# The cross loop's order on TensorE: the attended pair directly behind the third scores, and what follows from it

## What is computed

```python
z = _mha(x1, context, Wq2, Wk2, Wv2, mask1, causal=False)   # 16 heads of 32
x2 = _layernorm(x1 + z, ln2_g, ln2_b)
z = jnp.maximum(x2 @ fc1_w.T + fc1_b, 0.0) * mask0
z = (z @ fc2_w.T + fc2_b) * mask0
return _layernorm(x2 + z, ln3_g, ln3_b)
```

## Time and profile before

| | us |
|---|---|
| median of 3 runs | 2673.7 (2673.52 to 2676.07) |
| the profiled execution, its own time | 2674.73 |
| its span in the trace | 2673.0 |
| TensorE busy in the span | 2629.6 (98%) |
| VectorE busy in the span | 1911.7 (72%) |

### The profile page before, as it was taken

The page is one execution under the profiler, slowest core; times in us unless marked ns, Lnnn a source line. Parts: engine busy times, 40 slices in busy tenths (PEclk is TensorE's granted clock), DMA queues, the critical chain, the costliest instruction groups (busy, mean ns, idle before and its releaser), DMA issues.

```text
span 2673.0 us, 66075 instructions
## 1 busy us (share of the span) xinstructions
PE 2629.6 (98%) x22888; PEld 2268.3 (85%) x22888; DVE 1911.7 (72%) x5311; ACT 1546.2 (58%) x4774; POOL 744.7 (28%) x943
## 2 busy tenths in 40 slices
PE   7999999999999999999999999999999999999997
PEld 6888888887888888888888888888788888888886
DVE  7777877776534443444478888887788888888877
ACT  6777777777211111111267777777676776767764
POOL 3333343330100000000103333333442434424342
PEclk9999999999999999999999999999999999999998
DMA  4333334252211211022121111112321322213210
GB/s 157 119 121 98 110 111 127 87 156 78 89 54 41 61 36 60 31 63 63 48 96 48 47 47 47 47 47 79 100 80 63 98 67 71 86 63 99 66 50 23
DMA packets 180500, 202.54 MB, mean 76 GB/s; under 512 B 17616, under 2 KB 107728, under 8 KB 179536
## 3 DMA queue, kind: packets, MB, share of 16 engines
q1 hardware_dynamic: 180432, 201.66, 23.6%
HBM read 137.65 MB, written 63.96 MB: 75 GB/s over the span
## 4 chain that ended last, share of the span: by engine, by line
PE 93%; DVE 4%; ACT 2%; issue 1%; DMA 0%; POOL 0%; DVEq 0%; ACTq 0%; POOLq 0%
PE cross_work L172 17%; PE mlp_acc L3137 13%; PE mlp_f L3119 13%; PE mask_work L172 13%; PE causal_work L172 10%; PE cross_scores L2146 3%; PE mask_scores L2146 3%; PE cross_scores L2123 2%; PE causal_scores L2146 2%; PE mask_attended L2173 2%; PE cross_attended L2173 2%; PE mask_scores L2123 2%; PE causal_scores L2123 2%; PE causal_attended L2173 2%; PE cross_probsT L2146 1%; PE mask_probsT L2146 1%
## 5 line engine op out<-in xcount | busy, mean ns | idle before, releaser
L2915 ACT ACTIVATE mlp_h<-mlp_f,mlp_b1col 128x512 f32<-128x512 f32 x128 | 88.3, 690 | 526.1 <-PE mlp_f L3119 526.0
L3119 PE MATMUL mlp_f<-mlp_xT_hi,mlp_w 128*128 128x512 f32 x1024 | 335.4, 389 | 0.2 <-DVE mlp_xT_lo L3006 0.2
L3020 DVE CAST mlp_hT_hi<-mlp_h 128x512 fp32r<-128x512 f32 x128 | 58.1, 454 | 369.9 <-ACT mlp_h L2915 369.8
L3137 PE MATMUL mlp_acc<-mlp_w,mlp_hT_hi 128*128 128x512 f32 x1024 | 315.2, 389 | 0.0
L888 ACT ACTIVATE mask_prob<-mask_scores,mask_low 128x256 f32<-128x256 f32 x512 | 236.0, 486 | 66.0 <-DVE mask_low L1445 64.7
L888 ACT ACTIVATE cross_prob<-cross_scores,cross_low 128x256 f32<-128x256 f32 x512 | 237.3, 490 | 63.3 <-DVE cross_low L1439 63.3
L888 ACT ACTIVATE causal_prob<-causal_scores,causal_low 128x128 f32<-128x128 f32 (+1 forms) x512 | 210.4, 437 | 93.4 <-DVE causal_low L1445 93.4
L3119 PEld LDWEIGHTS mlp_f<-mlp_xT_hi,mlp_w 128*128 128x128 f32 x1024 | 192.1, 188 | 40.8 <-DVE mlp_xT_lo L3006 0.6
L1445 DVE CUSTOM_DVE_ANT_0 mask_scores<-mask_scores,mask_mask 128x256 f32<-128x256 f32 x512 | 198.6, 461 | 38.5 <-PE mask_scores L2123 27.7
L3137 PEld LDWEIGHTS mlp_acc<-mlp_w,mlp_hT_hi 128*128 128x128 f32 x1024 | 192.2, 188 | 39.8
L172 PE MATMUL causal_work<-causal_xT_hi,causal_w 128*128 128x256 f32 x1008 | 217.0, 293 | 0.3 <-DVE causal_qk_parts L1404 0.3
(11 more groups left out here) (350 smaller groups left out, 7808.9 us busy)
## 6 DMA issues: line engine op xcount, KB each, us to landing
cross_x_in<-after_attention SPq DMA_DIRECT2D x17, 512.0 KB, 4.1
mask_x_in<-in_x SPq DMA_DIRECT2D x16, 512.0 KB, 4.3
mask_c_in<-in_ctx SPq DMA_DIRECT2D x16, 512.0 KB, 5.2
mask_res<-in_x SPq DMA_DIRECT2D x16, 512.0 KB, 3.6
after_attention<-mask_res SPq DMA_DIRECT2D x16, 512.0 KB, 2.8
mlp_x<-after_attention SPq DMA_DIRECT2D x8, 1024.0 KB, 5.7
mlp_stage<-in_L_xattn_fc_w SPq DMA_DIRECT2D x8, 1024.0 KB, 5.6
after_layer<-mlp_y SPq DMA_DIRECT2D x8, 1024.0 KB, 4.3
```

The source lines that it names most:

```text
L2915: act.activation(h32[:, m % 2, :], F1[m % 2][:], ACT.Gelu, bias=b1col[:, m:m + 1]).then_inc(s["gelu"], 1)
L3119: ins = pe.matmul(F1[m % 2][:], W[2 * (m // 4)][:, a, k, m % 4 * P:(m % 4 + 1) * P], xT[p][:, k, :], start=(k == 0 and n == 0), stop=(k == ...
L3137: ins = pe.matmul(ACC[t][:], hT[a][:, m % 2, t * P:(t + 1) * P], W[2 * (m // 4) + 1][:, p, m % 4, :], start=(m == 0 and n == 0), stop=(m = ...
```

## The change

On TensorE the second values are made whole (twelve matmuls) between turn_probs(b,6) and turn_probs(b,7). The attended pair, attend(b,0,2), is issued directly behind scores(b,2), ahead of post_turn. The second post_turn writes bank W0, where the values stood, and not O; its wait is now for v_ready. turn_probs(b,8) and (b,9) stand ahead of feed1(b,0,(0,)), turn_probs(b,10) behind it. ScalarE takes values(b,1) directly behind turned(b+1,1), then exps(b,8), exps(b,9), and only then post_hi(b,0) and post_hi(b,1). VectorE makes the four minima of chunk 2 in one go ahead of post_lo, where two stood on either side. The turn of b = 0 keeps its work, with a small reordering; in cross_end the first of the four banks becomes O for W0.

```diff
-    POST_BANK = (W1, O) if cross else (SC[2], O)
+    POST_BANK = (W1, W0) if cross else (SC[2], O)
...
-    END_BANK = (W0, PT, SC[2], SC[3])
+    END_BANK = (O, PT, SC[2], SC[3])
...                                  (ScalarE, cross_turn)
-            if not prev:
-                values(b, 1)
-            if prev:
-                post_hi(b, 0)
-                post_hi(b, 1)
+            values(b, 1)
             if cur:
                 exps(b, 8)
-                if prev:
-                    values(b, 1)
...
                 exps(b, 9)
...
+                if prev:
+                    post_hi(b, 0)
+                    post_hi(b, 1)
                 exps(b, 10)
                 exps(b, 11)
                 copy(b, 8)
...                                  (VectorE, cross_turn)
-                minima(b, 2, (0, 1))
+                minima(b, 2)
             if prev:
                 post_lo(b, 0)
                 post_lo(b, 1)
-            if cur:
-                minima(b, 2, (2, 3))
...                                  (TensorE, cross_turn)
                 pe.wait_ge(s["v_ready"], 2 * b + 1)
-                values(b, 1, 0)
+                values(b, 1)
...
                 turn_probs(b, 7)
                 scores(b, 2)
+                attend(b, 0, 2)
...
                 post_turn(b - 1, 0)
-                pe.wait_ge(s["z_done"], KC * b + 1)
+                pe.wait_ge(s["v_ready"], 2 * b + 2)
                 post_turn(b - 1, 1)
             if cur:
                 energies0(b, 3)
-                if prev:
-                    values(b, 1, 1)
-
+            if cur and not prev:
+                pe.wait_ge(last["z_done"], KC * B + 1)
+                attend(b, 0, 2)
+            if cur:
+                turn_probs(b, 8)
+                turn_probs(b, 9)
             if prev:
                 feed1(b, 0, (0,))
             if cur:
-                if not prev:
-                    pe.wait_ge(last["z_done"], KC * B + 1)
-                attend(b, 0, 2)
-                turn_probs(b, 8)
+                turn_probs(b, 10)
             if prev:
                 feed1(b, 0, (1,))
-            if cur:
-                turn_probs(b, 9)
-
-            if cur:
-                turn_probs(b, 10)
-            pe.wait_ge(s["v_ready"], 2 * b + 2)
-            if prev:
                 feed1(b, 1, (0,))
                 attended(b, 0, 2)
                 feed1(b, 1, (1,))
```

## The result

The changed kernel takes 2727.43 us (median of 4 runs, 2726.42 to 2728.93) against 2673.93 us (4 runs, 2673.52 to 2676.07) for the kernel before: a ratio of 1.0197, with a 95% interval of 1.0185 to 1.0209 (the two medians alone give 1.0200). The prediction was 2727.3. Its span is 2726.4 us, 53.4 more than before.

The account below looks back on a forecast made before the run. TensorE was taken as full, with a path through VectorE equally long. The longer path's 3.8 us for b = 1 to 13, plus 3.0 and 1.2, summed to 53.6 us: 2727.3 us, range 2697 to 2738.

Parts of the forecast that it names:

- Two paths of equal length: TensorE's own list, and post_turn through post_hi and VectorE's list to qk_lo and queries(b+1,1), both close a turn, 0.07 us apart.
- TensorE's own list: TensorE's stream, full at 47.73 us a turn before; predicted to grow 1.7 us a turn.
- the path through VectorE: From the first post_turn through VectorE's list to queries(b+1,1): 3.8 us a turn longer, bounds 2.7 and 4.2.
- The three waits: New TensorE waits each turn: at attend 0.6 us, at feed1 for post_lo 0.4, at the attended pair's transposes 0.8.
- What VectorE is late with: TensorE waits at turn_probs(b,12), feed2 and queries(b+1,1), 2 us together.
- the reading by whole instructions: VectorE and GpSimd take turns at SBUF by whole instructions: 3.8 us a turn, 2727 us, chance 0.56.
- a mere sharing: VectorE and GpSimd only share SBUF bandwidth, so the early minima are a real gain: 2.7 us, 2712, chance 0.20.
- The sum: Whole loop: 49.4 us for b = 1 to 13, 3.0 for b = 14, 1.2 for b = 15; 53.6 us.
- The change of shape: One change of TensorE's array shape fewer per turn, saving 0.1 us, bounds 0 and 0.2.

Follow-up runs that it names:

- e3: Changed kernel with VectorE's copy of m0 moved ahead of the minima of chunk 2: 2717.75 us, 9.7 less than the changed kernel.
- e6: Changed kernel with ScalarE's attended moved ahead of relu(b,0): 2727.49 us, no change.
- e1: Changed kernel with ScalarE taking turned(b+1,1) and the second values ahead of copy 7: 2719.14 us, 8.3 less than the changed kernel.
- e2: Changed kernel with GpSimd's four residual instructions left out: 2700.82 us, ratio 1.0096 to the kernel before.
- e7: Changed kernel with values and turned ahead of copy 7, the residual's four instructions left out, and attended ahead of relu(b,0): 2687.64 us.
- e4: Changed kernel with the attended pair alone put back behind feed1(b,0,(0,)): 2727.39 us, as much as the changed kernel.

## Why the prediction was right, step by step

**The bound.** Two paths of equal length, with 0.07 us between. The control without the residual (2673.3) bears out TensorE's own list as the bound before, though only by the 0.14 us that it freed. That the path through VectorE had no slack before rests on the 0.07 us read in the trace: the values made whole (+20.5) don't show it, since there TensorE's own wait at feed1 gives nearly all of the loss. In the changed kernel VectorE's path is shown as the bound: its list made shorter takes 0.7 us off a turn (e3), a wait of TensorE's own taken out gives nothing (e6).

**The three waits.** Predicted 0.6, 0.4 and 0.8; found 0.62, 0.42 and 0.87 in the trace after. The first lies on the path that counts (e1: 8.3 us less), the third does not (e6: nothing); the second was not taken out by itself. What VectorE is late with was put at 2 us together and is 1.85, at the three places named.

**The path through VectorE.** Predicted 3.8 us a turn, found 3.69; the copy of m0 was to take 0.5 to 1.2 us and takes 1.26, a little more; GpSimd's four instructions were to end 7.2 us after the first post_turn and do so (2062.24 - 2055.03 = 7.21). Choosing the reading by whole instructions over a mere sharing was worth 15 us of the forecast, and rested on two rows of before: 0.77 against 0.16 us for one copy, and 2.98 against 2.53 us for a pair. The split minima (+2.9, not +16) bear that choice out, and so does the residual left out (e2: the pair of turned and the copy 2.7 us shorter).

**The sum.** Predicted 53.6, found 53.4 in the span. Its parts agree less well than the whole: 13 turns give 48.0 (49.4 predicted) and the one after 3.1 (3.0). The first post_turn is 4.8 us later than before (1952.19 against 1947.36); 3.9 of it were foreseen, and 1.0 is there already at scores(1,1), which come ahead of every edit of that turn (1939.48 against 1938.51), 0.7 of it from before the cross loop. Behind the last post_turn 2.4 us are won back; that attend and half of the values have been made already explains most of it, but no run shows it apart. Without that 1.0 the two ends give 4.8 - 1.0 - 2.4 = 1.4 us, where I had put 1.2 for the turn of b = 15. So the loop was taken 1.4 us too dear (3.8 us a turn, measured 3.69), and the 1.0 ahead of it makes up for most of that. That is luck: where the last matmul of the GELU block starts, up to which all twelve kernels are the same, their profiled executions differ by as much (1344.89 to 1346.56). The mechanism and the size of its terms were right; that the whole agrees to a few tenths of a us was not earned.

**The change of shape.** Predicted at 0.1 us a turn, and 0.1 is what is left when the waits of e7 are taken off.

**What was off** lies in the expectations of the experiments: e4's waits were about right by the turn (3.1 for 3.3 us), but not all that the whole loses lies in them; e7 and the control left out what becomes late next (relu); e3 gave the cut too long a wait.

## What to carry to other kernels

Where one engine is full, look up when each of its inputs is ready against when it is used, not how busy the others are: an engine that is busy for 72% can stand 0.07 us from the bound in every turn. A block of work on the full engine also covers the waits behind it. Moved ahead, it leaves the place where it stood without cover, and makes late what it now stands in front of. Of several new waits, those count that lie on the longest path. Before work is moved on VectorE, see what GpSimd does in the time it moves to: there an instruction on two columns can cost as much as a long one.

## What the runs showed of the hardware

A VectorE copy of 128x2 elements took 0.16 us where GpSimd was idle and 1.26 us beside a GpSimd instruction over 128x512, ending 0.03 us behind it; GpSimd's pair took 2.53 us with none, 2.98 with one and 3.44 with two of VectorE's turned between. The Trainium skill, SBUF — State Buffer, section SBUF: two separate sides, has this as a lock held for the whole instruction; these numbers agree. I had not foreseen that a cut that came 0.8 us ahead of the end of such a GpSimd instruction ended only 0.15 us behind it, though it takes 0.35 us alone: by these numbers some 0.2 us of it did not have to wait. VectorE's post_lo, which read one of their two large operands from PSUM, kept their time: 1.66 us for the four beside GpSimd, and 1.66 where the residual was left out.
